# Reordering the entry into linear attention: a normalisation placed two experts later, masked queries of the first batch made on VectorE, and the second batch projected between states and scores

## What is computed

```python
x = x + 0.5 * _L0_ffn_ref(_layernorm(x), ...)      # mixture of 8 experts, top 2     (moe_a)
x = x + _L0_attn_ref(_layernorm(x), ...)           # linear attention, 16 heads of 8 (linatt)
x = x + 0.5 * _L0_ffn_ref(_layernorm(x), ...)      # the same experts again          (moe_b)
x = x + 0.5 * _L1_ffn_ref(_layernorm(x), ...)      # gated feed-forward, FP4 values  (ffn_a)
x = x + _L1_attn_ref(_layernorm(x), ...)           # softmax attention               (att)
x = x + 0.5 * _L1_ffn_ref(_layernorm(x), ...)      # feed-forward again              (ffn_b)
```

```python
phi_q = relu(q) + EPS ;  phi_k = relu(k) + EPS
S   = cumsum(phi_k (outer) v, over the tokens)
out = (phi_q . S) / max(scale * pos, EPS)
return out @ proj_w.T
```

## Time and profile before

| | |
|---|---|
| runs, median (lowest to highest) | 740.05 us (737.7 to 740.06), 3 runs |
| profiled execution, its own time | 742.46 us |
| its span, first to last instruction | 740.5 us |
| mean granted TensorE clock | 0.971 of full speed |
| busy share PE / PEld / DVE / ACT / POOL | 90% / 65% / 82% / 62% / 40% |
| share of the chain that ended last | PE 64%, DVE 16%, ACT 10%, issue 6%, POOL 3% |

### The profile page before, as it was taken

The page is one execution under the profiler, slowest core; times in us unless marked ns, Lnnn a source line. Parts: engine busy times, 40 slices in busy tenths (PEclk is TensorE's granted clock), DMA queues, the critical chain, the costliest instruction groups (busy, mean ns, idle before and its releaser), DMA issues.

```text
span 740.5 us, 16304 instructions
## 1 busy us (share of the span) xinstructions
PE 666.4 (90%) x5826; PEld 478.0 (65%) x5826; DVE 605.3 (82%) x1554; ACT 458.3 (62%) x867; POOL 295.1 (40%) x417
## 2 busy tenths in 40 slices
PE   4999999979999999999996789999979978889995
PEld 2777776658788776777774556566647546556564
DVE  2688878746767688978786899999999999899983
ACT  3777777775576338777785476657544434576642
POOL 5000022056556501010013677554535538677520
PEclk9999999999999999999999799999999999999997
DMA  8000000000000000000000000000000000010100
GB/s 210 23 0 0 0 1 0 2 2 4 3 0 3 3 2 1 1 1 0 0 1 0 1 0 1 1 0 1 2 0 0 0 1 1 0 29 15 29 15 28
DMA packets 13463, 7.10 MB, mean 10 GB/s; under 512 B 1177, under 2 KB 13409, under 8 KB 13409
## 3 DMA queue, kind: packets, MB, share of 16 engines
q1 hardware_dynamic: 11328, 5.33, 2.7%
q10 hardware_dynamic: 2080, 1.05, 0.5%
HBM read 4.28 MB, written 2.10 MB: 9 GB/s over the span
## 4 chain that ended last, share of the span: by engine, by line
PE 64%; DVE 16%; ACT 10%; issue 6%; POOL 3%; DMA 1%; DVEq 0%; POOLq 0%; ACTq 0%
PE ps L1464 59%; DVE shared L1275 3%; DVE shared L1303 3%; PE ps L1859 2%; DVE x_sb L1100 2%; ACT ffn_work L536 2%; ACT ffn_work L737 2%; PE ps L1472 1%; ACT xnT L587 1%; ACT x_sb L846 1%; PE ps L1478 1%; ACT ffn_work L574 1%; DVE stats L1001 1%; ACT hqT L842 1%; ACT ffn_work L569 1%
## 5 line engine op out<-in xcount | busy, mean ns | idle before, releaser
L1464 PEld LDWEIGHTS ps<-w_sb,sq_h 128*128 128x128 f32 x1024 | 133.1, 193 | 71.1 <-ACT sq_h L606 51.0
L1100 DVE SCALAR_TENSOR_TENSOR x_sb<-ps,gates,x_sb 128x128 f32 (+1 forms) x512 | 147.0, 343 | 21.4 <-PE ps L1464 17.3
L1464 PE MATMUL ps<-w_sb,sq_h 128*128 128x128 f32 x1024 | 138.8, 279 | 3.3 <-ACT sq_h L606 3.3
L1464 PE MATMUL ps<-xnT,w_sb 128*128 128x512 f32 x256 | 134.9, 610 | 0.0
L602 ACT ACTIVATE relu_h<-ps 128x512 f32<-128x512 f32 x128 | 75.6, 590 | 57.8 <-PE ps L1464 57.5
L357 POOL TENSOR_SCALAR vareps<-meanvar 128x4 f32<-128x4 f32 (+1 forms) x28 | 8.9, 319 | 255.7 <-DVE meanvar L1010 255.3
L606 ACT ACTIVATE sq_h<-relu_h 128x512 f32<-128x512 f32 x128 | 80.6, 630 | 4.0
L1464 PE MATMUL ps<-gateT,xnT 128*128 128x352 f32 x128 | 58.9, 544 | 17.4 <-ACT ffn_work L737 13.0
L404 POOL TENSOR_TENSOR shared<-shared 128x128 f32<-128x128 f32 x112 | 51.5, 459 | 27.2 <-ACT shared L696 19.0
L580 ACT ACTIVATE xn<-x_sb,shift,rstd 128x128 f32 (+1 forms) x136 | 57.1, 481 | 6.5 <-POOL shift L365 5.6
L1464 PE MATMUL ps<-downT,hqT 128*128 128x128 f32 x384 | 57.4, 288 | 4.2 <-ACT hqT L842 4.0
(11 more groups left out here) (166 smaller groups left out, 1335.7 us busy)
## 6 DMA issues: line engine op xcount, KB each, us to landing
x_sb<-in_L_attn_x_dram SPq DMA_DIRECT2D x8, 256.0 KB, 7.1
out_dram<-x_sb SPq DMA_DIRECT2D x8, 256.0 KB, 2.3
w_sb<-in_L_ffn_w_all_dram ACTq DMA_DIRECT2D x2, 512.0 KB, 6.3
wraw<-in_L_attn_qkv_w_dram SPq DMA_DIRECT2D x1, 192.0 KB, 4.8
wraw<-attn_in_proj_weight_dram SPq DMA_DIRECT2D x1, 192.0 KB, 3.7
fraw<-in_L_ffn_w_down_dram SPq DMA_DIRECT2D x1, 176.0 KB, 3.1
fraw<-in_L_ffn_w_gate_dram SPq DMA_DIRECT2D x1, 128.0 KB, 2.7
fraw<-in_L_ffn_w_up_dram SPq DMA_DIRECT2D x1, 128.0 KB, 2.5
```

The lines of the kernel that those rows point to most:

```text
L1100: t = nc.vector.scalar_tensor_tensor(tile_b(i, j), bank(4 + e % 4, TPB, C)[:, j, :], gates[:, j, e:e + 1], tile_b(i, j), ALU.mult, ALU.add)
L1464: return nc.tensor.matmul(o, a, b, start=start, stop=stop, **kw)
```

## The change

Six edits, all around the end of moe_a's last batch and the start of linatt.

1. ScalarE normalises batch 0 of linatt after experts 1 and 2 of moe_a's last batch (before: after expert 7 of the batch ahead, and expert 0). Its transposes on TensorE move from expert 1 to 3, the copy-out from 2 to 4, the key projection from 3 to 5 and the query projection from 4 to 5, queries_out from 5 to 6, and VectorE's moments of batch 1 and its `keys` by one expert each.
2. ScalarE normalises batch 1 in one piece after expert 7, not in halves after 6 and 7.
3. q_bd of batch 0 is made by four VectorE instructions instead of ScalarE's four; they stand ahead of VectorE's moments of batch 2.
4. TensorE transposes batch 1 ahead of states(0), and ScalarE copies it out ahead of take_states(0).
5. TensorE projects keys and queries of batch 1 between states(0) and scores(0), no longer after scores(0).
6. In body 0, VectorE masks the third quarter of the scores before it makes phi_k of batch 1, since phi_k of batch 0 must be read first.

No engine's work becomes less or more, except that four instructions change their engine.

```diff
--- before.py
+++ after.py
@@ -617,17 +617,19 @@
 
                             n = (e - 2) * TPB // 2
                             normalise(s, i + 1, n, tile_b, n - TPB // 2)
-                        if not more and e == 0:
+                        if not first and not more and e == 0:
                             normalise(nxt, 0, TPB, tile_n, TPB // 2)
                         if first and not more:
+                            if e == 1:
+                                normalise(nxt, 0, TPB // 2, tile_n)
                             if e == 2:
+                                normalise(nxt, 0, TPB, tile_n, TPB // 2)
+                            if e == 4:
                                 evac_xnT(nxt, 0)
-                            if e == 5:
+                            if e == 6:
                                 queries_out(nxt, 0)
-                            if e == 6:
-                                normalise(nxt, 1, TPB // 2, tile_n)
                             if e == 7:
-                                normalise(nxt, 1, TPB, tile_n, TPB // 2)
+                                normalise(nxt, 1, TPB, tile_n)
                         if not first and not more:
                             if e == 3:
                                 x_squares(nxt, 0)
@@ -646,7 +648,7 @@
                                 fp4_weight_out(e - 1)
                             if e == 5:
                                 fp4_weight_out(2)
-                        if known_after(i, GROUPS - 2) and more and e == 7:
+                        if not first and known_after(i, GROUPS - 2) and more and e == 7:
 
                             normalise(nxt, 0, TPB // 2, tile_n)
                         if e == 6 and more:
@@ -683,6 +685,9 @@
                     nc.scalar.activation(v_tok[:, side, :, :], bank(2, TPB, C), ACT.Copy).then_inc(s["vtok_ready"], 1)
                     act.wait_ge(s["kT_done"], i + 1)
                     nc.scalar.activation(k_tok[:, :, :], bank(3, TPB, C), ACT.Copy).then_inc(s["ktok_ready"], 1)
+                    if type(i) is int and i == 0:
+                        evac_xnT(s, 1)
+                        return
                     act.wait_ge(s["phiq_ready"], i + 1)
                     for hh in range(HQ):
                         nc.scalar.activation(q_bd[:, side, hh, :], phi_q[:, :], ACT.Copy,
@@ -715,7 +720,6 @@
                 front(0, 0)
                 act.wait_ge(s["state_zero"], 1)
                 take_states(0, 0)
-                evac_xnT(s, 1)
                 linatt_bodies(act, body)
 
             def normal(s, first, g):
@@ -1116,10 +1120,10 @@
                             else:
                                 ln_stats(nxt, ch, 0, TPB, tile_n)
                         if not more and first:
-                            if e == 2:
+                            if e == 3:
                                 dve.wait_ge(nxt["xn_ready"], 1)
                                 ln_stats(nxt, ch, 1, TPB, tile_n)
-                            if e == 4:
+                            if e == 5:
                                 keys(nxt, 0)
                             if e == 6:
                                 queries(nxt, 0)
@@ -1212,9 +1216,14 @@
 
                 def body(i, side):
                     more = known_below(i, GROUPS - 1)
-                    if more:
-                        keys(s, i + 1)
-                    scores(i, 2, side)
+                    if type(i) is int and i == 0:
+
+                        scores(i, 2, side)
+                        keys(s, 1)
+                    else:
+                        if more:
+                            keys(s, i + 1)
+                        scores(i, 2, side)
                     scores(i, 3, side)
                     if more:
                         queries(s, i + 1)
@@ -1244,6 +1253,10 @@
                         w4.scales()
                     pick(i, 1, side)
 
+                dve.wait_ge(s["phiq_ready"], 1)
+                for hh in range(HQ):
+                    nc.vector.tensor_scalar(q_bd[:, 0, hh, :], phi_q[:, :], headsel[:, hh:hh + 1], None,
+                                            ALU.mult).then_inc(s["qbd_ready"], 1)
                 dve.wait_ge(s["xn_ready"], 2)
                 ln_stats(s, ch, 2, TPB, tile_b)
                 scores(0, 0, 0)
@@ -1558,12 +1571,11 @@
                             transposes(s, i + 1)
                         if first and not more:
 
-                            if e == 1:
+                            if e == 3:
                                 transposes(nxt, 0)
-                            if e == 3:
+                            if e == 5:
                                 pe.wait_ge(s["sub_ready"], GROUPS)
                                 keys_in(nxt, 0)
-                            if e == 4:
                                 queries_in(nxt, 0)
                             if e == 6:
                                 pe.wait_ge(s["relu_done"], E * i + E - 1)
@@ -1599,11 +1611,6 @@
             def linatt(s, nxt, follow):
                 router, up, down, _ = follow
 
-                def project_in(i):
-                    keys_in(s, i)
-                    queries_in(s, i)
-                    values_in(s, i)
-
                 def turn_keys(i):
                     pe.wait_ge(s["phik_ready"], i + 1)
                     if type(i) is not int or i > 0:
@@ -1690,7 +1697,10 @@
                 def body(i, side):
                     more = known_below(i, GROUPS - 1)
                     if more:
-                        project_in(i + 1)
+                        if type(i) is not int or i > 0:
+                            keys_in(s, i + 1)
+                            queries_in(s, i + 1)
+                        values_in(s, i + 1)
                         turn_keys(i + 1)
                     if not more:
 
@@ -1721,11 +1731,13 @@
                         down(0, 0)
 
                 turn_keys(0)
+                pe.wait_ge(s["reluq_ready"], 1)
+                transposes(s, 1)
 
                 pe.wait_ge(S["moe_a"]["out_free"], 4 + E * (GROUPS - 1) + 6)
                 states(0, 0)
-                pe.wait_ge(s["reluq_ready"], 1)
-                transposes(s, 1)
+                keys_in(s, 1)
+                queries_in(s, 1)
                 scores(0, 0, 0)
                 scores(0, 0, 1)
                 linatt_bodies(pe, body)
```

## The result

Twelve runs of the changed kernel and twelve of the kernel before, interleaved on one chip, have medians of 737.72 and 742.57 us and give a ratio of 0.9941 (95% interval 0.9923 to 0.9960): 0.59% faster. Put on the 740.05 us of the three runs known ahead of the prediction, that is 735.7 us, where 736.2 was forecast (ratio 0.9948). That there is a gain is clear; whether it is above 0.5% the interval leaves open, as it holds gains of 0.40% to 0.77%. The profiled execution took 739.65 us with a span of 737.3, against 742.46 and 740.5.

A forecast was written before the change was run, and what follows sets the result against it. TensorE's two waits and the lower clock behind each bound this place. 4.6 us at across(0) plus 0.95 behind it minus 1.7 for the clock make 3.85 us, so 736.2 us; 8-in-10 range 734 to 739.

The forecast's parts named there:

- What bounds it: Around moe_a's end and linatt's start: TensorE's waits of 2.36 and 2.8 us, each with 1.72 us lost to the clock.
- Edit 1: End of moe_a: the 2.36 us wait and 1.72 us lower clock go, turn_keys(0) 4.08 us earlier.
- the rival in which VectorE comes only 2 us earlier: First wait only exchanged, VectorE 2 us earlier and not 3.6: gain 2.2 us, 737.8 us; chance 0.06.
- Edits 2 and 4: Start of linatt: 0.1 us allowed for the later normalisation, copy-out free, states(0) 4.0 us earlier.
- Edits 3 and 5: Between states(0) and scores(0): projections fit between, masks don't delay TensorE, scores(0) 4.9 us earlier.
- The prefix is late next: GpSimd's prefix sums, 150.5 to 158.4 us: TensorE waits 2.6 us, across(0) still starts 4.6 us earlier.
- Behind it: After across(0): of the 1.15 us wait of scores(1) for ScalarE's taken states, 0.95 us go.
- The clock: After the new wait of 2.6 us ahead of across(0): one stretch at the lower clock, 1.72 us lost.
- To the end: Body 1 onward: starts about 4 us earlier, and the same shift stands at every later place.
- No lower stretch: Rival: the clock doesn't fall after the prefix wait; gain 5.6 us, 734.5 us; chance 0.14.
- A long one: Rival: a long lower clock stretch loses 1.5 to 3.5 us more; 737.7 to 739.7 us; chance 0.18.
- The lock between VectorE and GpSimd: Rival: they block one another, each masked query takes 1.6 us; 0.8 us slower, 740.8 us; chance 0.04.

The follow-up runs named there:

- e1: Kernel before with only the moe_a part changed (ScalarE's normalisation of batch 0 later, of batch 1 in one piece); ratio to before 0.9952.
- e5: Changed kernel with keys and queries of batch 1 projected behind scores(0) again; ratio to before 0.9954.
- e8: Second run of the kernel of e4 (changed kernel, masked queries back on ScalarE); one run, across(0) 14.52 us after turn_keys(0).
- e6: Changed kernel with batch 0's 14 prefix adds on 8 of 128 columns, the rest left out; ratio to before 0.9882.
- e3: Changed kernel with VectorE's moments of batch 2 ahead of its four masked queries of batch 0; ratio to before 0.9917.
- e2: Kernel before with only the new linatt entry (masks on VectorE, batch 1's transposes and projections early), moe_a as before; ratio to before 1.0009.
- e4: Changed kernel with batch 0's masked queries back on ScalarE, ahead of the taken states; ratio to before 0.9932.
- e10: The kernel of e3 measured again, beside the changed kernel; median 735.26 us, ratio to before 0.9895.
- e7: Changed kernel with an unused 128x4096 memset on GpSimd just ahead of VectorE's masks; one run, across(0) 16.51 us after turn_keys(0).

## Why the prediction was right, point by point

**What bounds it.** Right. TensorE's two waits and the lower clock behind them were the price at this place. e1 takes away the first with its stretch, and that alone brings batch 2 forward by 4.1 us of the 4.7.

**Edit 1.** Forecast 4.08 us at turn_keys(0), measured 3.95 (147.94 to 143.99). The exponential began at 131.62 (131.7 forecast), VectorE's gates at 131.95, 3.57 earlier (3.6), and its last accumulation ended at 145.47 (145.3). So the rival in which VectorE comes only 2 us earlier is out. e1 shows that edits 1 and 2 are most of the gain: 4.14 of the 4.72 us at batch 2.

**Edits 2 and 4.** states(0) 3.90 us earlier, forecast 4.0.

**Edits 3 and 5.** scores(0) at 149.35, forecast 149.15. The masks took 1.68 us, inside the 1.3 to 2.9 allowed, below the 1.8 that I took. Single ones were 0.48 us long, as the row of this kernel had it (0.49), and not the 0.33 us estimated from the Trainium skill's formula (VectorE: DVE Perf Modes, The TRN2 errata). e5 and e8 show something that the forecast priced only together. Against this prefix, taking back edit 5 alone moves across(0) by 0.02 us, and taking back edit 3 alone by 0.18 (e8); in e1, which has none of edits 3 to 6, it comes 0.8 later. Edits 4 and 6 were not tried alone.

**The prefix is late next.** Right, and the step on which the size hung: start 150.44 (150.5), 7.83 us (7.87), across(0) at 158.33 (158.45), TensorE's wait 2.30 (2.6). e6 takes the prefix away, and the wait goes; e3 moves it by 1.07 us, and across(0) moves by 1.07. What the prediction says of the other order was too much: it puts the cost of having the masks first at 1.8 us and the wait without it below 1 us. e3 measured 1.07 and 1.25 us, since there the taken states start the prefix and not ln_group(2).

**Behind it.** This term was too small. I put 0.95 us. From across(0) to batch 2 it took 9.31 us before and 9.31 after, though the second holds 1.7 us of lost clock. So about 1.7 us of waits went: the 1.15 for the taken states, of which I had left 0.2 standing, and a pause of 0.65 inside across(0) that the prediction doesn't have. These are the two in the kernel before, and across(0)'s second half in the changed one:

```profile
166.46 1.11 PE L1464 MATMUL ps<-shared,phi_k 32*32 32x128 f32 x61 [1.15 <-issue]
...
170.29 1.05 PE L1464 MATMUL ps<-shared 128*128 128x128 f32 x8 [0.65 <-issue]
```

```profile
164.58 2.05 PE L1477 MATMUL ps<-shared 128*128 128x128 f32 x16
```

That is 1.80 us, against which a new wait of 0.23 stands ahead of within(0).

**The clock.** There is one stretch of 1.7 us behind the new wait, as forecast, in both profiles of the changed kernel. The sum at batch 2 is then 4.72 us, not 3.85. That a wait of this length has just this price is not a rule: e2's cost 6.8.

**To the end.** The shift doesn't stay the same at every place, as I had written that it should, and I had named a change of it in later stages as a sign that the forecast is wrong. This step failed in the profile: 1.7 us more were lost to the clock from 254 to 262, and of 4.72 us 3.2 were left at the end. The average over the runs does better. The measured 0.59% is 4.4 us. The loss by the clock (span times one minus granted clock) is 21.5 us in the profile before and 21.4 in the profile after; over the twelve runs of the changed kernel it is 19.0, and over the 24 runs of the kernel before beside e1 to e4 it was 20.4.

**How much of it is luck.** The mechanism was right at each place up to across(0). That 735.7 lies only 0.5 us from 736.2 is luck in part: the sum at batch 2 was 0.9 us too small, mostly by the term behind across(0), and later stages took 1.5 us from the shift in the profile. The interval of the ratio stands for a gain of 3.0 to 5.7 us and couldn't tell these apart.

**The rivals.** No lower stretch: not so here, but so in e3 and e10, where the wait is 1.25 us, and in e6, where there is none. A long one: not in the changed kernel, but in e2, at the same wait (6.8 us lost). The lock between VectorE and GpSimd: real, as e7 shows, and without effect here, since GpSimd is idle while the masks run (6.37 us until the moments are there). By e7 its price isn't what the rival had: one block for the memset that runs, not one for each mask. Of the two rows that the prediction calls in agreement with the rule on a tensor_scalar, only the one of 1602 ns is of that form; the add of 0.94 us ran beside a SCALAR_TENSOR_TENSOR.

## What to carry to other kernels

Before an engine is relieved of work on one path, ask which queue the work lands in and what stands behind it there. The four masks left ScalarE's way to the scores and stood on VectorE ahead of moments that GpSimd's slowest chain waits for. Putting those moments first cost nothing, as scores(0) started 5.35 us after turn_keys(0) in e3 and 5.36 in the changed kernel, and it gave 2.8 us more in time.

A wait of TensorE costs its length and what its clock loses with it, here mostly 1.7 us. Shortening one wait, with the clock then staying up (e3, e10), paid more than moving it to another place (e5). Where such a stretch falls is not a property of the edit alone, so an edit of 1 us has to be read at a fixed place in the trace, counted from a fixed start, and in more than one profile.

## What the runs showed of the hardware that I had not expected

- The same order of instructions ran twice, with the clock falling at 151 us once (5.1 us lost to 162) and at 162.9 the other time (e4, e8). With a prefix wait of 2.3 us it was low for 3.4 us in the changed kernel and for some 14 in e2. In the changed kernel it fell 0.6 us after TensorE had gone on, in e2 0.8 us before.
- The clock also fell behind short waits: at 162.9 in e8, 1.6 us after one of 0.83 us had ended, and a second time at 166.2 in e7, 1.2 us after one of 0.70 us. e3 and e10 have the wait of 0.83 us too, and there it didn't fall.
- In the second half of across(0) TensorE stands still for 0.4 to 0.7 us, with no releaser in the profile, in the kernel before, e1, e5 and e6. These are the four in which scores(1) waited 1.0 to 1.15 us for the taken states just ahead of it. In the other eight profiles there is neither that wait nor the pause. What holds TensorE there I haven't found out.
- GpSimd's adds take long however small they are: 14 adds on 8 columns took 4.39 us, 0.31 each with the wait for the one before, and on 128 columns 7.83, 0.56 each. By these numbers, halving the count of adds should shorten the prefix more than halving their columns; that was not tried.
